# Softmax weights divided before their transposes, values as the stationary operand, and a reordered step in the local-attention stream of a fused kernel

## The reference, cut to what matters

```python
qkv = h @ wqkv
q, k, v = jnp.split(qkv, 3, axis=-1)          # 8 heads of 64
q = l2norm(q) * qs
k = l2norm(k) * ksc
q, k = rotary_xpos(q, k)
...
sim = jnp.einsum('bhwid,bhwjd->bhwij', bq, bk)    # windows of 64 queries, 128 keys
sim = jnp.where(mask, -jnp.finfo(sim.dtype).max, sim)
attn = jax.nn.softmax(sim, axis=-1)
out = jnp.einsum('bhwij,bhwjd->bhwid', attn, bv)
...
x = x + o @ wo
```

## Time and profile before

| | before |
|---|---|
| median of three executions | 1000.57 us |
| the profiled execution, its time | 1000.6 us |
| its span in the profile | 998.5 us |
| mean granted TensorE clock | 0.996 |
| PE busy | 939.0 us (94%) |
| DVE busy | 732.4 us (73%) |
| ACT busy | 728.0 us (73%) |
| POOL busy | 386.4 us (39%) |

### The profile page before, as it was taken

How to read it: one execution, slowest core, us unless ns; L and a number is a source line. 1 busy time by engine, 2 the same in 40 slices (tenths; PEclk the granted TensorE clock), 3 DMA queues, 4 the chain that set the end, 5 groups by cost and what they waited for, 6 DMA issues and landing times.

```text
span 998.5 us, 22947 instructions
## 1 busy us (share of the span) xinstructions
PE 939.0 (94%) x8744; PEld 575.5 (58%) x8744; DVE 732.4 (73%) x1218; ACT 728.0 (73%) x1563; POOL 386.4 (39%) x272
## 2 busy tenths in 40 slices
PE   8999999999789999999999999999999999999985
PEld 4333333333566676666766566666666666766752
DVE  6887878886487777777777677777677777777741
ACT  3577777778688786877867677777778868788662
POOL 2110113123366536455443534434355454544411
PEclk9999999999999999999999999999999999999999
DMA  2210100000211101011000101000011011110100
GB/s 82 66 40 10 26 2 2 3 1 2 59 29 28 24 18 33 18 28 23 18 23 17 23 18 23 17 13 22 18 23 29 18 26 25 23 39 17 34 22 11
DMA packets 23303, 23.72 MB, mean 24 GB/s; under 512 B 8626, under 2 KB 15068, under 8 KB 23196
## 3 DMA queue, kind: packets, MB, share of 16 engines
q1 hardware_dynamic: 23196, 22.27, 9.3%
HBM read 6.16 MB, written 1.05 MB: 7 GB/s over the span
## 4 chain that ended last, share of the span: by engine, by line
PE 54%; DVE 10%; ACT 5%; issue 3%; POOL 1%; DVEq 0%; POOLq 0%; ACTq 0%
PE psum L1381 8%; PE psum L1350 6%; PE psum L1292 5%; PE psum L1389 4%; PE psum L1313 4%; PE psum L1302 3%; PE psum L1264 3%; PE psum L1253 3%; DVE BS L1619 3%; PE psum L1374 3%; PE psum L1255 3%; PE psum L1254 3%; DVE A L1615 3%; PE psum L1368 2%; PE psum L1277 2%
## 5 line engine op out<-in xcount | busy, mean ns | idle before, releaser
L1182 POOL TENSOR_TENSOR A<-A,BS 128x1024 f32<-128x1024 f32 x62 | 146.2, 2359 | 207.1 <-DVE BS L1619 206.9
L878 DVE TENSOR_REDUCE a_M<-psum 128x2 f32<-128x1024 f32 x128 | 155.3, 1220 | 34.0 <-PE psum L651 33.2
L1187 POOL TENSOR_TENSOR A<-A,RN 128x1024 f32<-128x1024 f32 x62 | 117.9, 1902 | 89.5 <-ACT RN L1511 86.0
L1496 ACT ACTIVATE f_PW<-psum,f_NM 128x128 f32<-128x128 f32 x512 | 138.5, 381 | 18.7 <-DVE f_NM L1651 18.7
L774 ACT ACTIVATE a_PT<-psum 128x1024 f32<-128x1024 f32 x128 | 128.8, 1020 | 23.2 <-PE psum L661 23.0
L1615 DVE TENSOR_TENSOR A<-psum,cos 128x512 f32<-128x512 f32 x124 | 84.8, 684 | 35.1 <-ACT SQ L1462 35.1
L1651 DVE TENSOR_REDUCE f_NM<-psum 128x4 f32<-128x512 f32 x128 | 82.1, 683 | 38.5 <-PE psum L1292 38.5
L1462 ACT ACTIVATE SQ<-psum 128x512 f32<-128x512 f32 x124 | 72.1, 624 | 49.4 <-PE psum L1255 46.4
L1381 PE MATMUL psum<-f_mid,w 128*128 128x512 f32 (+1 forms) x192 | 87.0, 603 | 2.7 <-DVE f_mid L1681 2.7
L1313 PEld LDWEIGHTS psum<-f_VS,f_PT 128*64 128x64 f32 x1024 | 64.5, 137 | 38.8 <-issue 38.3
L1619 DVE TENSOR_TENSOR BS<-psum,sin 128x512 f32<-128x512 f32 x124 | 84.2, 679 | 0.0
(11 more groups left out here) (212 smaller groups left out, 1946.1 us busy)
## 6 DMA issues: line engine op xcount, KB each, us to landing
f_VS<-V SPq DMA_DIRECT2D x112, 130.0 KB, 2.3
raw<-L_ffn_wqkv_dram SPq DMA_DIRECT2D x2, 768.0 KB, 4.8
a_XT<-L_attn_a_x_dram SPq DMA_DIRECT2D x4, 256.0 KB, 2.9
out_dram<-f_OUT SPq DMA_DIRECT2D x4, 256.0 KB, 2.3
w<-L_ffn_w_dram SPq DMA_DIRECT2D x2, 341.0 KB
tables<-const_dram SPq DMA_DIRECT2D x1, 512.0 KB, 3.7
wo<-L_ffn_wo_dram SPq DMA_DIRECT2D x8, 64.0 KB
const<-const_dram SPq DMA_DIRECT2D x1, 264.0 KB, 3.1
```

The lines of the kernel that those rows point to most:

```text
L878: nc.vector.tensor_reduce(M[:, quads % 2, t, 2 * j:2 * j + 2], psum[:, pair("scores", i), :], AX_X, ALU.max).then_inc(s("maxed"), 1)
L1182: nc.gpsimd.tensor_tensor(A[:, k % 2, :, :], A[:, k % 2, :, :], BS[:, k % 2, :, :], ALU.add)\
L1187: nc.gpsimd.tensor_tensor(x, x, RN[:, k % 2, :, None].to_broadcast([P, 2 * HW, DW]), ALU.mult)\
L1496: last = nc.scalar.activation(PW[:, u % 4, c, :], psum[:, bank("scores", u), P * c:P * c + P], ACT.Exp, bias=NM[:, u % 4, c:c + 1])
```

## The change

The weights are now divided by their sums before they are transposed. A new stage `weigh` (lag 2) does it: DVE reduces `PW` of a whole tile (128 x 1024 elements) to eight sums and takes the reciprocal, POOL multiplies `PW` in place. The ones column, `ON`, the two divisions and the stage `turn_o` go. `sums` now has the values as stationary operand and `PT` as moving one (64 columns), so it gives features by tokens at once, into one bank instead of two; ACT copies that bank into `OT`. The output weights are loaded in their natural order of heads. In the table, `turn_p` and `sums` have lag 3 instead of 2; both transposes open PE's step, `sums` stands right behind `project`, and on ACT the copy of `PT` opens the step, with `values` and the copy of `OT` ahead of `turn`.

```diff
 STEP = {
-    "PE": [("latent", 8, of_sequence),
-           ("project", 0, of_tile), ("features_b", 10, of_sequence), ("turn", 1, of_tile), ("features_a", 1, of_first), ("project_a", 2, of_first),
-           ("context", 9, of_sequence),
-           ("turn_o", 3, of_tile), ("project_b", 10, of_sequence), ("w1", 5, of_group), ("turn_p", 2, of_tile), ("turn_p_2", 2, of_tile),
+    "PE": [("latent", 8, of_sequence), ("turn_p", 3, of_tile), ("turn_p_2", 3, of_tile),
+           ("project", 0, of_tile), ("features_b", 10, of_sequence), ("sums", 3, of_tile), ("turn", 1, of_tile),
+           ("features_a", 1, of_first), ("project_a", 2, of_first), ("context", 9, of_sequence),
+           ("project_b", 10, of_sequence), ("w1", 5, of_group),
...
+    "POOL": [("lead", 0, of_lead), ("split", SEQS, of_tile), ("weigh", 2, of_tile), ("scale", 0, of_tile), ("w2", 6, of_group),
...
+                    elif stage == "weigh":
+                        k = i
+                        pool.wait_ge(s("den_recip"), k + 1)
+                        x = PW[:, 2 * (k % 2):2 * (k % 2) + 2, :, :].rearrange("p u c x -> p (u c) x")
+                        nc.gpsimd.tensor_tensor(x, x, RD[:, k % 2, :, None].to_broadcast([P, 2 * PAIRS, P]), ALU.mult)\
+                            .then_inc(s("weighed"), 1)
...
                 def turn_p(u):
-                    pe.wait_ge(s("exped"), u + 1)
+                    pe.wait_ge(s("weighed"), u // 2 + 1)
...
+                    dst = take("sums", k).rearrange("p (c x) -> p c x", c=PAIRS)
+                    pe.wait_ge(s("p_copied"), k + 1)
+                    pe.wait_ge(s("p_copied_2"), k + 1)
+                    for c in range(PAIRS):
+                        for w, values in ((0, VS), (1, V)):
+                            for j in range(2):
                                 last = nc.tensor.matmul(
-                                    dst[WIN * w:WIN * w + WIN, c, :], PT[:, u % 4, c, WIN * w:WIN * w + WIN],
-                                    values[:, k % 4, 2 * c + j, :], start=True, stop=True)
...
+                                    dst[DW * j:DW * j + DW, c, WIN * w:WIN * w + WIN],
+                                    values[:, k % 4, 2 * c + j, :],
+                                    PT[:, (2 * k + j) % 4, c, WIN * w:WIN * w + WIN], start=True, stop=True)
+                    last.then_inc(s("sums"), 1)
...
+                    elif stage == "weigh":
+                        k = i
+                        dve.wait_ge(s("exped"), 2 * k + 2)
+                        if k >= 2:
+                            dve.wait_ge(s("weighed"), k - 1)
+                        x = PW[:, 2 * (k % 2):2 * (k % 2) + 2, :, :].rearrange("p u c x -> p (u c) x")
+                        nc.vector.tensor_reduce(RD[:, k % 2, :], x, AX_X, ALU.add).then_inc(s("den"), 1)
+                        dve.wait_ge(s("den"), k + 1)
+                        nc.vector.reciprocal(RD[:, k % 2, :], RD[:, k % 2, :]).then_inc(s("den_recip"), 1)
```

More of the change, by code:

```diff
@@ L219, in row @@
                     return a[name][layer:layer + 1]
[L221 removed]
                 todo += [
[L223 to L224 removed]
+                    (g.wo[:, layer, :, :], row("L0_ffn_wo").rearrange("a (c p) n -> p (a c) n", p=P)),
                     (g.w1[:, layer, :], row("L0_ffn_w1").rearrange("a p n -> (a p) n")),
@@ L994 @@
            ("var_mlp", 4, of_group), ("var_a", 3, of_first), ("var_b", 7, of_sequence),
-           ("var_y", 10, of_sequence), ("w2", 6, of_group), ("wo", 3, of_group), ("sums", 2, of_tile), ("store", 6, of_end)],
-    "ACT": [("latent", 8, of_sequence),
-            ("squares", 0, of_tile), ("features_b", 10, of_sequence), ("turn", 1, of_tile), ("features_a", 1, of_first), ("values", 0, of_tile), ("turn_o", 3, of_tile),
+           ("var_y", 10, of_sequence), ("w2", 6, of_group), ("wo", 3, of_group), ("store", 6, of_end)],
@@ L998 @@
+    "ACT": [("turn_p", 3, of_tile), ("latent", 8, of_sequence),
+            ("squares", 0, of_tile), ("features_b", 10, of_sequence), ("values", 0, of_tile), ("sums", 3, of_tile),
+            ("turn", 1, of_tile), ("features_a", 1, of_first),
             ("center_mlp", 4, of_group), ("center_a", 3, of_first), ("center_b", 7, of_sequence),
-            ("center_y", 10, of_sequence), ("split", SEQS, of_tile), ("w1", 5, of_group), ("turn_p", 2, of_tile), ("keys_b", 8, of_sequence),
+            ("center_y", 10, of_sequence), ("split", SEQS, of_tile), ("w1", 5, of_group), ("keys_b", 8, of_sequence),
@@ L1051, in stream @@
             order += [("turned_q", i), ("turned_k", i)]
-        elif stage in ("scores", "sums", "keys_b", "tokens_b"):
+        elif stage in ("scores", "keys_b", "tokens_b"):
             order += [(stage, 2 * i), (stage, 2 * i + 1)]
@@ L1063, in stream @@
             order += [("var", number[stage[4:], i])]
-        elif stage in ("turn_o", "wo", "w2", "context", "features_b", "project_b", "store", "features_a", "project_a"):
+        elif stage in ("sums", "wo", "w2", "context", "features_b", "project_b", "store", "features_a", "project_a"):
             order += [(stage, i)]
@@ L1342, in _ @@
                         sums(i)
-                    elif stage == "turn_o":
-                        turn_o(i)
                     elif stage == "wo":
@@ L1527, in _ @@
                         nc.scalar.activation(OT[:, :, P * t:P * t + P],
-                                             psum[:, bank("turn_o", k), :].rearrange("p (c x) -> p c x", c=PAIRS),
+                                             psum[:, bank("sums", k), :].rearrange("p (c x) -> p c x", c=PAIRS),
                                              ACT.Copy).then_inc(s("o_copied"), 1)
```

64 lines of the change are left out of this document (16 added, 48 removed).

## The result

The changed kernel takes 1039.32 us (median of 4 runs, 1033.47 to 1045.68) beside 1000.67 us for the kernel before: ratio 1.0385, 95% interval 1.0323 to 1.0448. The forecast was 1004.9 us, its range 997 to 1014: the sign was right, the size was missed by 34 us. The profiled execution is the fastest of the four (1033.47 us, span 1031.6, mean granted clock 0.974; the others have 0.962 to 0.970).

A forecast was written before the change was run, and what follows sets the result against it. PE was taken to set the pace. Plain groups -3, B stretch +2.1, start +2.1, end +3.0 and its group +0.1 gave +4.3 us on 1000.6: 1004.9 us, range 997 to 1014.

The forecast's parts named there:

- the copy of `KT`: w2 and wo steps: the scores wait 0.5 to 0.7 us for it, as nothing stands between `turn` and the masks.
- `sums` wait for the copy of `PT`: Plain groups: PE waits 0.3 us in the w2 step and 0.8 in the w1 step for ACT's copy.
- The bank waits: PE's waits for banks the rotation still reads, 10.5 us over 330 to 960 us, vanish: ten banks a tile, not twelve.
- 1.0 us later for X: B groups: X reaches the norm after `project_b` 1.0 us later, behind DVE's new work; four times, +4.0 us.
- 0.7 for `latent`: Next-to-last gap of each B group: `latent` queued behind `weigh` on DVE delays a norm's bank; 0.7 us each, +2.8.
- the B stretch: Stretch with the four B groups: +4.0 and +2.8 us of delays, -4.7 in its other gaps, together +2.1 us.
- Plain groups: Four gaps of -0.1, -0.3, -0.4 and +0.4 us: 41.77 becomes 41.4 us, -0.4 each, -3 us over eight groups.
- Start: Three weight-splitting steps: `weigh` on POOL between split and rotation, up to 1.9 us each, 5.7 in all; taken as +2.1.
- Steps of the last call and the end: Two store-step groups -0.3 us; from last masks to last output projection +3.0 us, from lag 3 and a later preceding tile.
- The first: Rival: PE stays the bound, 28.2 us and up to 10.5 us of bank waits return: 962 to 972 us; chance 0.12.
- The third: Rival: PE waits for POOL, rotated q and k late in one gap of four: 1015 to 1022 us; chance 0.1.
- the fourth: Rival: the two halves of `sums` no longer overlap, +1 us a tile: 1065 us; chance 0.02.

The follow-up runs named there:

- r2: r1 with `sums` moved behind `turn` in PE's order: 999.15 us, ratio 0.9971 to the kernel before.
- r3: The changed kernel without the division (no reduction, reciprocal or product): 1012.11 us, ratio 1.0124 to the kernel before.
- r4: The changed kernel without GpSimd's product alone, sums and reciprocals still computed: 1029.35 us, ratio 1.0265 to the kernel before.
- r7: The changed kernel with four spare matmuls in the two long PE waits of each B group: 1025.08 us, ratio 1.0231 to the kernel before.
- r8: The changed kernel with `latent` ahead of `weigh` on VectorE: 1027.8 us, ratio 1.0247 to the kernel before.
- r9: r5 with ScalarE's copy of OT moved to the head of its step: 964.92 us, ratio 0.9643 to the kernel before.
- r1: The changed kernel with ScalarE's copies of `QT` and `KT` ahead of those of V and OT: 1043.84 us, ratio 1.0419 to the kernel before.
- r5: The changed kernel put back in the old order, keeping swapped operands and no `turn_o`, without the division: 1014.85 us, ratio 1.0119 to the kernel before.

## Why the prediction was right in sign and wrong in size

**Right.** What PE is freed from does not come back with this order, since `turn` directly ahead of the masks leaves the copy of `KT` uncovered and `sums` wait for the copy of `PT`. Both waits are there, at the steps named. r2 shows that the cover was it: put back, the plain group is 39.29 us, 2.9 less. The bank waits vanished, GpSimd's product holds nothing in plain steps (r3 and r4 leave them at 42.21), `sums` without a wait costs its 1.08 us, and X is waited for 2.4 us where I said 2. (By my own gaps eight plain groups were to gain 3.4 us and not the 3 of the sum; it changes nothing.)

**The step that failed: no term for TensorE's clock.** I priced each wait at its own length: 1.0 us later for X and 0.7 for `latent`, +6.8 in the B stretch, +2.1 net. The waits grew about so (from 1.06 to 2.38 and from 1.2 to 2.05). What I left out is that behind seven of the eight waits the matmuls ran at 1.2 GHz: r7 removes that without moving the producers, and 11.1 of the stretch's +13.8 us go. In r7 the B stretch takes 262.4 us (506.64 to 769.03), +2.7 over before, where I had +2.1. For `latent`, the mechanism was right and the size off: r8 measures 2.1 us for it in the three groups where the clock had fallen, and 0.6, the wait itself, in the one where it had not. The clock is the largest single term, 11.1 of the 28.6 us that the forecast missed in this execution, but not the whole: r7, at 1025 us, still lies above my range, and what remains is the sizes below. The median lies 5.9 us above the profiled execution; all that the record shows for that is its lower mean clock.

**Plain groups, a size: -0.4 forecast, +0.43 measured.** Four small prices were missing, all read from the chain of the after kernel, and not tested one by one. From the end of ScalarE's copy of `PT` in the chain to the start of `sums` it takes 0.25 us, 0.74 from the copy's start where I had 0.64. `sums` behind a wait takes 1.15 (0.07 more), the scores behind a wait 1.10 (0.23 more, twice a group), `turn` behind `sums` 1.02 (0.15 more). Their sum is more than the 0.85 that is missing; I take it that a part of them falls where PE would have waited for ScalarE anyway. I had taken each duration from a row in which the engine came straight from other work. Counted from start to start on the timeline the differences are smaller: the scores 1.04 us behind a wait (381.99 to 383.03) and 0.97 otherwise (402.73 to 403.70), `sums` 1.08 and 1.09. The rest is that without a wait a group starts before the modelled end of the one in front (scores at 402.73, masks to 402.90), and behind a wait it cannot.

**Start, a size: +2.1 forecast, +6.0 measured.** I had bounded the split steps at 5.7 and taken +2.1. GpSimd's product stands behind the split, and PE waits for it:

```profile
289.78 1.97 PE L1304 MATMUL psum<-const,f_PW 128*128 128x128 f32 x8 [2.61 <-POOL f_PW L1189]
300.88 1.09 PE L1304 MATMUL psum<-const,f_PW 128*128 128x128 f32 x8 [2.61 <-POOL f_PW L1189]
```

The eight transposes of the first take 1.97 us where the second's take 1.09: the clock again (0.50 over 290 to 292 us). r3 (-7.0) and r4 (-4.5) point to the division for nearly all of it, most of that GpSimd's product; since single executions differ by up to 6 us at this tick, the shares are rough.

**Steps of the last call and the end: +2.7 forecast, +10.1 measured** (the last three lines of the table). The two groups with a store step lose 2.0 us each, 0.4 of it as every plain group and most of the rest in the wo gap (11.20 us, against 9.89 without a store; before, 9.94 against 10.05): the store's transposes now stand right behind the w2 matmuls and wait for X, where `sums` lay between them before. I did not look at what `sums` had covered at its old place. At the end, in the after kernel:

```profile
992.85 0.48 PE L1315 MATMUL psum<-f_PT,f_VS 128*64 128x64 f32 x4 [2.69 <-ACT f_PT L1507]
...
998.97 0.66 PE L1439 MATMUL psum<-const,X 128*128 128x128 f32 x4 [0.85 <-DVE X L1694]
...
1001.37 0.34 PE L1315 MATMUL psum<-f_PT,f_VS 128*64 128x64 f32 x4 [0.88 <-DVE f_PT L1632]
...
1003.21 3.70 PE L1339 MATMUL psum<-f_OT,wo 128*128 128x512 f32 x8 [0.69 <-ACT f_OT L1516]
```

The 2.69 us wait is three times that of a w1 step (0.93), and the `sums` behind it run at the slower clock (0.48 for a piece that takes 0.34 at 1001.37). The mean granted clock behind the last projection is 0.80 (1003 to 1031 us) against 0.92 before (971 to 998); how much of the 1.5 us that is was not tested.

**The rivals.** The first, 962 to 972 us, was wrong for this order; r9, at 964.9, shows the price of the removed work, but without the division. The rule of the Trainium skill ("Perfetto Trace Analysis", Identifying the Most-Contended Engine), to optimize the engine with the highest occupancy first, stood behind this rival, and the runs bear it out only where the order lets PE run: r9 gains, the after kernel loses. The third (GpSimd as the gate) has its mechanism in the start only; the fourth is out. None of them held the clock, and so no case of mine reached 1039.

## What to carry to other kernels

Before an operation is moved, ask what it covers at its old place, and what covers its result's copy at the new one: one entry moved in an order gave 45 us here (r2 against r1), one copy 50 us (r9 against r5), more than the work that the change removes. Price a wait of TensorE by its length only while it is as short as those that the profile already shows at full clock; if it grows from 1 to 2 us, read the granted clock, since the half-speed stretch behind it can cost more than the wait (here 0.6 us of waiting made 2.1). Read it in several executions, as the same wait is not followed by the slow clock each time. And where a result has a single bank that is taken again some uses later, follow the copy that frees it as closely as the one that uses it.

## What the runs showed of the hardware

- In the after kernel, seven of the eight waits of 2.05 and 2.38 us were followed by matmuls at half speed; waits of 1.06 and 1.2 at the same places before, and of 1.44 in other runs, were not (mean granted clock over 500 to 750 us 0.95, in r7 without the long waits 1.00). With the earlier wait at 1.44 us, the same 2.38 us wait was followed by it in 6 of 16 groups only, and the 3.31 us wait at 980.59 not at all, though the same wait in r1, r3, r7 and r8 was (granted clock 0.50 to 0.71 over the 3 us behind it). The four executions of the after kernel differ by 12 us, in step with their mean clock (0.974 at 1033.47 us, 0.962 at 1045.68).
- Four spare matmuls per B group, 16 in all, made the kernel 14.2 us faster by the medians, and the stretch that they stand in 11.1 us shorter.
- The first matmuls behind a wait cost extra at full clock too, as the chain counts them: 32 scores 1.10 us against 0.87, 32 of `sums` 1.15 against 1.08. From start to start it is 1.04 against 0.97 and 1.08 against 1.09.
- Eight transposes behind `sums` (values stationary, 64 output partitions each) take 1.02 us in the chain, against twice 0.44 in the earlier trace rows. That the change of shape on PE costs it was not tested by itself.
